# The first expert in three pieces, the second in two, each finished and stored right behind its ReLUs

## The reference, cut to what matters

```python
t = _to_tokens(x)                                   # 4096 x 64, after the first layer
h = _ln_t(t)
idx = argmax(softmax(h @ gate_w + gate_b))          # one expert a token
pos = rank of the token among those of its expert   # kept if pos < C = 640
buf[idx, pos] = h                                   # 8 x 640 x 64
hmid = relu(buf @ w1 + b1)                          # up:   64 -> 256
ybuf = hmid @ w2 + b2                               # down: 256 -> 64
y = ybuf[idx, pos] * (prb * kept)
out = t + nan_to_num(y, nan=0, posinf=1e4, neginf=-1e4)
```

## Time and profile before

| | us |
|---|---|
| median of 3 runs | 378.38 (378.09 to 379.71) |
| profiled execution | 379.07 |
| its span | 377.3 |
| GpSimd busy | 278.4 |
| VectorE busy | 307.1 |
| TensorE busy | 302.6 |
| TensorE's mean granted clock | 0.888 |

### The profile page before, as it was taken

The page is one execution under the profiler, slowest core; times in us unless marked ns, Lnnn a source line. Parts: engine busy times, 40 slices in busy tenths (PEclk is TensorE's granted clock), DMA queues, the critical chain, the costliest instruction groups (busy, mean ns, idle before and its releaser), DMA issues.

```text
span 377.3 us, 4331 instructions
## 1 busy us (share of the span) xinstructions
PE 302.6 (80%) x1257; PEld 178.5 (47%) x1257; DVE 307.1 (81%) x352; ACT 232.6 (62%) x519; POOL 278.4 (74%) x198
## 2 busy tenths in 40 slices
PE   7842788847988898998899697579988689999950
PEld 3321333213634344464436254436476357888940
DVE  5799999999999999999999979899998215755620
ACT  4455989623888984688898419856655145646320
POOL 3345669888894899989599988699997604477772
PEclk9975699996998989889899879989999759999985
DMA  4879999987999798859959685999961090000000
GB/s 92 146 173 359 321 343 324 300 270 241 275 295 339 295 320 304 257 178 340 364 146 341 219 242 136 339 304 341 217 107 31 20 276 12 4 20 16 22 12 0
DMA packets 48625, 78.68 MB, mean 209 GB/s; under 512 B 16210, under 2 KB 31373, under 8 KB 48602
## 3 DMA queue, kind: packets, MB, share of 16 engines
q1 hardware_dynamic: 46362, 76.54, 66.1%
q0 software_dynamic: 2240, 1.86, 1.6%
HBM read 72.30 MB, written 7.54 MB: 212 GB/s over the span
## 4 chain that ended last, share of the span: by engine, by line
DVE 56%; PE 18%; issue 10%; POOL 7%; ACT 3%; DMA 3%; DVEq 1%; POOLq 1%; ACTq 0%; SPq 0%
DVE h L1342 34%; DVE Bp L1289 15%; PE Cp L1162 5%; PE Bp L1176 4%; POOL slots L576 2%; POOL prod L534 2%; PE Yp L993 2%; POOL out_dram L626 2%; PE Bp L1151 1%; DMA csb<-slots 1%; DMA xs_in<-in_x_dram 1%; PE Yp L1193 1%; DVE h L1457 1%; POOL h L605 1%; PE Yp L1220 1%
## 5 line engine op out<-in xcount | busy, mean ns | idle before, releaser
L534 POOL TENSOR_TENSOR prod<-h,csb 128x1024 f32<-128x1024 f32 (+1 forms) x64 | 143.6, 2251 | 19.4 <-DVE h L1342 9.5
L993 PE MATMUL Yp<-prod,ident 128*128 128x512 f32 (+1 forms) x256 | 127.3, 634 | 13.7 <-POOL prod L534 13.5
L1342 DVE TENSOR_TENSOR_SCAN h<-dA,Bp 128x1024 f32<-128x1024 f32 (+2 forms) x58 | 119.7, 2064 | 4.9 <-POOL prod L534 1.2
L993 PEld LDWEIGHTS Yp<-prod,ident 128*128 128x128 f32 x256 | 50.6, 209 | 75.1 <-issue 51.3
L706 ACT ACTIVATE dA<-delta,aneg 128x1024 f32<-128x1024 f32 (+1 forms) x58 | 62.9, 1092 | 19.0 <-DVE h L1342 14.7
L1289 DVE TENSOR_TENSOR Bp<-Cp,bsb 128x1024 f32<-128x1024 f32 (+1 forms) x58 | 67.7, 1168 | 2.3
L626 POOL DMA_INDIRECT out_dram<-dA,csb x30 | 30.5, 1017 | 27.8 <-DVE dA L1533 20.8
L576 POOL DMA_INDIRECT slots<-rows_,slot x30 | 30.1, 1005 | 9.8 <-issue 5.4
L1521 DVE TENSOR_TENSOR dA<-Bp,b2s 128x320 f32<-128x320 f32 (+1 forms) x8 | 3.8, 475 | 22.0 <-PE Bp L1176 22.0
L1162 PE MATMUL Cp<-prod,w1s 128*128 128x384 f32 (+1 forms) x64 | 21.6, 462 | 0.0
L1176 PEld LDWEIGHTS Bp<-w2s,prod 128*128 128x128 f32 x152 | 18.1, 192 | 1.8 <-issue 0.3
(11 more groups left out here) (289 smaller groups left out, 592.0 us busy)
## 6 DMA issues: line engine op xcount, KB each, us to landing
bsb<-bc_rows SPq DMA_DIRECT2D x48, 512.0 KB, 6.1
csb<-bc_rows SPq DMA_DIRECT2D x48, 512.0 KB, 5.9
bsb<-bc_rows SPq DMA_DIRECT2D x16, 384.0 KB, 5.5
csb<-bc_rows SPq DMA_DIRECT2D x16, 384.0 KB, 5.1
csb<-slots SPq DMA_DIRECT2D x6, 325.0 KB, 5.2
slots<-fill SPq DMA_DIRECT2D x1, 1300.0 KB, 10.1
slots<-fill SPq DMA_DIRECT2D x10, 130.0 KB, 6.3
bcs<-bc_rows SPq DMA_DIRECT2D x2, 512.0 KB, 13.5
```

The costliest lines, as they stand in the source:

```text
L534: po.tensor_tensor(prod[:, k % 4, c], h[:, k % 3, c], csb[:, k % CSLOTS, c], ALU.mult).then_inc(s_pP, 1)
L993: ins = te_.matmul(Yp[:, c], idn, prod[:, k % 4, c], start=False, stop=(n == 15), skip_group_check=True)
L1342: ins = ve.tensor_tensor_scan(h[:, k % 3, c], decays, drives, h[:, k % 3, c.start - 1:c.start] if i else 0.0, ALU.mult, ALU.add)
```

## The change

`CHUNKS` becomes a list of seventeen: the first expert's three blocks are split in one and two. The transposes keep the old list, now `TURNS`, so the first two chunks share one turn. `FINISH` has five early pieces (one, two and two blocks of the first expert, three and two of the second), and then whole experts. On TensorE the first five chunks are written out: `up`, the next `turn`, and `down` of the same chunk. The semaphore counts follow. Pieces with index 1 and 3 write `Yp`. On ScalarE `back(LAST, 14)` stands ahead of `channels(0)`, and each further `channels` right ahead of a `hidden`; on VectorE `back(LAST, 15)` stands behind the second `finish`. `BEHIND` becomes 9, so the dense block begins at the same blocks as before.

```diff
-CHUNKS = [(e, k0, k1) for e in range(E) for k0, k1 in ((0, 3), (3, ET))]
+TURNS = [(e, k0, k1) for e in range(E) for k0, k1 in ((0, 3), (3, ET))]
+CHUNKS = [(0, 0, 1), (0, 1, 3)] + TURNS[1:]
-FINISH = [(0, 0, 3), (0, 3, ET)] + [(e, 0, ET) for e in range(1, E)]
-BEHIND = 8
+EARLY = 5
+FINISH = CHUNKS[:EARLY] + [(e, 0, ET) for e in range(2, E)]
+BEHIND = 9
...
-            return (Yp if i == 1 else Bp)[:, HALF:HALF + (k1 - k0) * C]
+            return (Yp if i in (1, 3) else Bp)[:, HALF:HALF + (k1 - k0) * C]
...
             def channels(i):
-                e, k0, k1 = CHUNKS[i]
+                e, k0, k1 = TURNS[i]
                 act.wait_ge(e_tr, i + 1)
                 if e >= 2:
-                    act.wait_ge(e_up, 2 * (i - 3))
+                    act.wait_ge(e_up, 2 * (i - 2))
...
                 if e >= 2:
-                    act.wait_ge(e_dn, e)
+                    act.wait_ge(e_dn, 3 if e == 2 else e + 2)
...
+            back(LAST, 14)
             channels(0)
-            channels(1)
-            back(LAST, 14)
             for i in range(len(CHUNKS)):
-                if 2 <= i + 1 < len(CHUNKS):
-                    channels(i + 1)
+                if 1 <= i < len(TURNS):
+                    channels(i)
                 hidden(i)
...
             def up(i):
                 e, k0, k1 = CHUNKS[i]
-                pe.wait_ge(e_xT, i + 1)
+                pe.wait_ge(e_xT, max(i, 1))
...
             def down(i):
                 e, k0, k1 = FINISH[i]
-                done = i + 1 if i < 2 else 2 * e + 2
+                done = i + 1 if i < EARLY else 2 * e + 3
                 pe.wait_ge(e_h0, done)
                 pe.wait_ge(e_h1, done)
                 if i == 1:
                     pe.wait_ge(b_yg, V)
                 elif i:
-                    pe.wait_ge(e_y, i)
+                    pe.wait_ge(e_y, i - 1 if i < EARLY else i)
...
             turn(0)
-            for i in range(len(CHUNKS)):
-                if i + 1 < len(CHUNKS):
-                    turn(i + 1)
-                if i == 1:
-                    down(0)
+            up(0)
+            turn(1)
+            down(0)
+            up(1)
+            back(LAST, 15)
+            turn(2)
+            down(1)
+            up(2)
+            turn(3)
+            down(2)
+            up(3)
+            turn(4)
+            down(3)
+            up(4)
+            turn(5)
+            down(4)
+            for i in range(EARLY, len(CHUNKS)):
+                e, k0, k1 = CHUNKS[i]
+                if EARLY < i < len(TURNS):
+                    turn(i)
                 up(i)
-                if i == 0:
-                    back(LAST, 15)
-                if i == 1:
-                    down(1)
-                if i >= 4 and i % 2 == 0:
-                    down(i // 2)
+                if e >= 3 and k0 == 0:
+                    down(FINISH.index((e - 1, 0, ET)))
...
             finish(0)
+            finish(1)
             back(LAST, 15)
-            for i in range(1, len(FINISH)):
+            for i in range(2, len(FINISH)):
                 finish(i)
```

More of the change, by code:

```diff
@@ L1181, in dense_turn @@
                 pe.wait_ge(b_hx, 1)
-                pe.wait_ge(e_y, 2)
+                pe.wait_ge(e_y, EARLY - 1)
                 for t in range(LT):
@@ L1266, in _ @@
                     dense_down(i - BEHIND - 1)
-            down(E)
+            down(len(FINISH) - 1)
             for j in range(len(CHUNKS) - BEHIND, BLOCKS):
```

## The result

The changed kernel takes 382.76 us (median of 6 runs, 381.81 to 386.01) against 378.66 for the kernel before on the same chips: a ratio of 1.0122, 95% interval 1.0081 to 1.0164. It is slower by 4.1 us, over the upper end of the range by 0.8. The profiled execution took 381.81, with a span of 379.9. The ratios further down leave out two runs, 383.22 us in experiment 1 and 380.40 in experiment 3, each over 1.5% above the fastest run of its kernel.

A forecast was written before the change was run, and what follows sets the result against it. GpSimd's row of stores was taken to set the end, its eleventh store held by TensorE reaching the third expert's products. That store moves from 331.92 to 332.29, so 378.38 + 0.37 = 378.75 us, range 377.3 to 382.0.

The forecast's parts named there:

- the clock: On TensorE, the low clock level, taken to end at 310.1 as before, costs the new order 1.5 us.
- The clock rises later: Rival: TensorE's clock stays low through the first expert (381.4) or the second's first up-products (382.7); chance 0.32.
- The sum at full clock: TensorE's five chunks of the first two experts: 1.61 + 2.64 + 2.64 + 3.58 + 2.64 = 13.11 us.
- The sum at the old clock: TensorE with the rise at 310.1: third expert's products begin at 323.65 + 1.5 = 325.15; time 378.75.
- The end: Third expert's products to chain end 6.35 us, then 0.79 to GpSimd: eleventh store at 332.29 against 331.92, +0.37 us.
- The eleventh store decides: On GpSimd, the third expert's first store goes when TensorE gets to that expert's products, whatever the first ten stores do.
- The hole moves and doesn't close: GpSimd's wait of about 4 us moves from the sixth store to the eleventh; chance 0.60.
- The first store: GpSimd's first store goes near 311.6, 3.7 us earlier than before.
- The one block: The first, one-block piece: finish chain on VectorE 1.88 us, ReLU on ScalarE 0.36 us.
- Free moves: ScalarE's exponential (0.20 us) and VectorE's gate step (0.88 us if uncovered) move at no cost.
- The dense block: The other ending, 1.45 us later, covered by 5 us; as rival it sets the end, over 383, chance 0.03.
- The hole closes: Rival: TensorE is not the holder, GpSimd's stores run without the 3.7 us hole, 371.0; chance 0.05 for 1.9 or more.

The follow-up runs named there:

- experiment 1: Changed kernel plus ten filler products in TensorE's gaps, nine ahead of the first turn and one behind it: 377.17 us, ratio to before 0.9957.
- experiment 3: Changed pieces, finishes and stores, but each chunk's up-products one chunk ahead of the down-products on TensorE, no fillers: 375.76 us, ratio to before 0.9908.
- experiment 8: Changed order with the pieces of before (first three blocks not split), ScalarE's copy of the next chunk behind the ReLUs: 379.13 us, ratio to before 1.0008.
- experiment 6: Changed kernel plus one filler product in each of four ReLU gaps on TensorE, none ahead of the tail: 378.81 us, ratio to before 1.0013.
- 4: Kernel of experiment 3 plus the fillers of experiment 1: 374.00 us, ratio to before 0.9877.
- experiment 7: Kernel of 4 with the third expert in two pieces as well: 373.14 us, ratio to before 0.9872.
- experiment 2: Kernel before, its order unchanged, plus the same fillers as experiment 1: 376.67 us, ratio to before 0.9939.

## Why the prediction was wrong

The step that failed is **the clock**: "Up to 310.1 the new order pays". It kept the moment of before for the clock's rise, and so charged 1.5 us for the low level. The change moved that moment to 319.7. What it then cost, from the starts of the up-products after, against the prediction's chunks: first chunk 2.65 us, predicted 1.61 + 0.40 + 0.46 = 2.47; second 4.37, predicted 2.64 + 0.63 = 3.27; third 4.36 against 2.64; fourth 4.95 against 3.58; fifth 2.61 against 2.64. Together 4.34 too little. That is the gap: the third expert's products begin 24.69 us after the first turn, predicted 325.15 - 304.66 = 20.49, so 4.20 late. The rest is that the first up-products began 0.09 sooner and that the stretch from the third expert's up-products to its down-products was 0.05 shorter.

The right mechanism stood among the rivals, as "The clock rises later", with 0.32 and a price of 381.4 for a clock low through the first expert and 382.7 through the second expert's first up-products. The second is what happened, and 382.76 was measured; at TensorE its price, 2.7 + 1.3 = 4.0 us, is near the 4.20. The reason I gave against it, that the gaps don't grow at the low level, was beside the point: from the second chunk on gaps hardly show in the trace at that level (0.18 us in front of the third chunk's down-products), and the clock stayed low without them. The Trainium skill's rule that was named there (Perfetto Trace Analysis, section Matmul Optimizations: matmuls back-to-back in batches) would have decided rightly for the change; for the kernel of experiment 8, which takes the batches apart in the same order and loses nothing, it would not.

The other steps held, with one term too long. *The sum at full clock:* in experiment 1 the third expert's up-products begin 13.16 us after the first ones (305.43 to 318.59), 13.11 in the sum. *The sum at the old clock:* experiment 6 brings the rise back to 5.2 us after the first turn, and its time, 378.81, is the forecast's 378.75. That they agree to 0.1 is partly luck: its third expert's products begin 0.26 later after the first turn than in the sum (20.75 against 20.49), and the next term is too long by a little more. *The end:* from the products to the eleventh store the sum has 6.35 + 0.79 = 7.14; measured 6.80 after (328.13 to 334.93) and in experiment 6.

*The eleventh store decides:* it waits 3.99 after, 3.93 and 4.00 with the clock mended. *The hole moves and doesn't close:* shown by the same rows; only where other products stand between up and down (3, 4) does it shrink to 1.95. The sign that no hole of that size stands in front of the sixth store came out less well: 3.12 after, 1.14 with the clock mended (1, 6). *The first store:* 6.99 us after the first turn, 6.94 worked out.

*The one block:* finish chain 1.73 us (307.80 to 309.53), 1.88 worked out; ReLU 0.37, 0.36 worked out. *Free moves:* ScalarE's exponential ended before its copy could start, VectorE's gate step lay in front of a wait of 1.18 us. *The dense block* stayed ahead, its store at 370.13, but only by 2.8 us.

*The hole closes* was given 0.05 for this change, and it didn't. That another order on TensorE, one more expert in pieces and the clock held up could close it, experiment 7, was not asked.

## What to carry to other kernels

Before cutting a chain of products into pieces, look at the granted clock where the first piece falls: if it is low there, its rise is a term of the sum that the change itself can move, and it can be worth more (here 4 us) than the wait that was to be saved. Keep other products between a piece's up and down: in this kernel the same pieces one chunk ahead gained 0.9% where behind their own ReLUs they lost 1.2%. And when a queue's hole is closed, find the next item's own limit first; here 1.08 us was all the hole could give.

## What was not expected of the hardware

Products of pure waste make this kernel faster: ten around the start of the tail gave 0.6% to the kernel before, whose order was unchanged, and four in the ReLU gaps took the changed one from 382.76 to 378.81. TensorE, shown 94% busy from 304 to 320, can stand at the lower level for nearly all of it, and shown 86% busy (experiment 2) at the higher level for all of it. Behind the short pieces the clock rose only when up-products of three blocks ran (they began at 316.21, the rise was at 319.7), as in before (306.55 and 310.1); with the products of another chunk between (3), or one filler (6), it rose without them. What in this mix raises it was not tried further and stays open.
